# Two layernorms' inverse roots in the third layer: from one GpSimd power each to twelve VectorE instructions

## The chip, the cores and the metric

The kernel runs on one core of a Trainium2 chip. The time is the device time of one execution in microseconds; several executions of a kernel give a median. The core's engines work side by side, each with an instruction stream of its own in a fixed order, and meet only through semaphores: TensorE (PE, the matmuls), VectorE (DVE), ScalarE (ACT), GpSimd (POOL) and SyncE (SP, which only issues transfers). Indirect gathers, with rows picked by a list, are issued by GpSimd.

## The reference

The program is a network of four layers on 64 graphs of 128 nodes with 128 features, and each layer has a graph part and a feed-forward part. The change lies in the graph part of the third layer. Cut to what matters, that part and what stands around it compute:

```
# second layer, feed-forward: gates come from an attention over 524288 edges
scores = layernorm(segment_sum(h[src] * alpha, dst) + b_gat).mean over heads
x = x + sum_e gate[e] * expert_e(x)
# third layer, graph part, per node
h = layer_norm(x)                    # (x - mean) * rsqrt(var + eps); "lift", twice in a row
x = layer_norm(h' + relu(adj @ h @ W_rel + h @ W_root + b))   # "settle"
# third layer, feed-forward: a shared expert, and the best 2 of 8 routed experts
x = x + shared(x) + sum over the top two of weight * expert(x)
# fourth layer: another normalization ("ease"), attention, another norm ("blend"), experts again
```

A layernorm needs the inverse root of a variance for every node. On the chip 128 nodes lie on the 128 partitions, so a tile of roots has 128 rows and one column for each graph (twice as many for `lift`, which folds two norms in a row into one pair of factors).

## The kernel before

The program has an early part (first two layers, up to about 1543 us) and `phase_c`, the rest. In phase C the 64 graphs are worked on in 8 turns of 8 graphs (`PAIR`), each turn in 2 groups of 4 graphs (`GT`), 16 groups in all. A piece of work is a task with a name and a number, and the tasks that matter here are these:

- `rows` (GpSimd: gathers of edge rows) and `edge` (VectorE, with ScalarE): the second half of the edge attention, 16 batches. The gathers for a batch wait until the batch two before it is used. `late` (VectorE: `settle_half`, L252, and `half_gates`, L2815) turns the sums into gates for the upper 32 graphs. Turns 4 to 7 can't begin before it.
- `sum` (VectorE): adds the gated experts of the second layer to a turn. `lift`, `lift_end`, `climb`, `enter_end`: the first norm of a turn. `adj`, `xt` (transposes at L429), `agg`, `conv` on TensorE; `settle` and `settle_end`: the second norm, of a group. `f2_score`, `route`, `mark`, `list`: routing.
- `pull` (GpSimd, two gathers at L2161): fetches the tokens of an expert pass. `flip` (TensorE, L2332) transposes them, `raise` is the first matmul of a pass and `lower` the second (both recorded at L2207), and `take` (VectorE, L2623) reads the result. There are two sets of banks, so `lower` number m waits for `take` number m - 2. There are 170 routed passes and 32 of the shared expert. `gather` and `gather_last` (GpSimd, L2176) fetch the results back, four gathers a task; `ease` and `blend` are the two norms of the fourth layer.

The first half of a norm is `measure` on VectorE: mean and variance by hardware statistics, then variance plus epsilon. The root was made by `invert` on GpSimd, at L2149, a power of -0.5, and VectorE waited for it in `set_factors`, where mean and root become the factors that ScalarE applies. `inverse_root` (L235) is a helper that exists already and is used in `half_gates`; every one of its instructions waits for the one before it (`link`).

The order in which each engine works through its tasks is not written by hand: `engine_orders` (L676) is a greedy planner. It takes for each task a list of engines with estimated durations (`LONG`, L1848), the tasks that it needs (`work_c`), and a worth: the length of the longest chain behind the task, plus offsets from a table (`PREFER_C`, L1864). From these it simulates the five engines and fixes one order for each. The table `LONG` thus sets the order of the whole phase.

## Time and profile before

| | us |
|---|---|
| median of 3 runs | 2917.36 |
| lowest and highest of them | 2911.76, 2921.22 |
| the profiled execution | 2921.49 |
| its span in the trace | 2919.7 |
| TensorE busy | 2277.4 (78%) |
| VectorE busy | 1896.5 (65%) |
| ScalarE busy | 1348.5 (46%) |
| GpSimd busy | 1326.9 (45%) |

The profiled execution is one more run, with the hardware profiler on; its time and its span differ by what lies before the first and after the last instruction. The granted TensorE clock was 0.881 of full speed on average. The busy shares are averages over a program whose stages have different limits, so they don't by themselves say what a change in one stage is worth.

### The profile page before, as it was taken

The numbers are of one execution on the slowest core, as the hardware profiler recorded it, in microseconds if no ns is written. First come the engines' busy times: TensorE is split into PE (matmuls) and PEld (weight loads), VectorE is DVE, ScalarE is ACT, GpSimd is POOL, SyncE is SP. The second block draws the span as 40 slices with busy tenths as digits, with TensorE's granted clock in tenths as the row PEclk, the third lists the DMA queues.
The fourth block names the chain that finished last, engine by engine and source line by source line (L and its number), as shares of the span: only waits on it lengthen the run. The fifth ranks groups of instructions, "written<-read, shape, count | busy, mean of one in ns | idle before, by whom it ended". The sixth has DMA issues, their size and how long they took to land. (4 is left out here: it accounts for less than half of the span.)

```text
span 2919.7 us, 41767 instructions
## 1 busy us (share of the span) xinstructions
PE 2277.4 (78%) x12088; PEld 1682.4 (58%) x12088; DVE 1896.5 (65%) x4776; ACT 1348.5 (46%) x2980; POOL 1326.9 (45%) x1219
## 2 busy tenths in 40 slices
PE   4887898989888979687741617578999998999990
PEld 3443454545545445455531516568888888898980
DVE  5989988776878757555467674387465476665312
ACT  3444556554646444344421515345646544454440
POOL 1120101010101066656774667722745747767776
PEclk9988989989898979899975758689999999999995
DMA  4010101000100021422223224134635536565772
GB/s 151 1 38 0 31 1 31 4 27 1 31 5 27 18 44 29 122 78 72 73 53 114 57 65 107 38 98 115 173 92 148 163 82 183 144 152 148 180 163 75
DMA packets 282613, 228.68 MB, mean 78 GB/s; under 512 B 90042, under 2 KB 234412, under 8 KB 281468
## 3 DMA queue, kind: packets, MB, share of 16 engines
q1 hardware_dynamic: 247580, 179.75, 21.2%
q0 software_dynamic: 34784, 46.03, 8.2%
q8 instruction: 104, 1.70, 0.2%
q14 instruction: 145, 1.19, 0.1%
HBM read 163.20 MB, written 63.70 MB: 78 GB/s over the span
## 5 line engine op out<-in xcount | busy, mean ns | idle before, releaser
L983 POOL TENSOR_TENSOR a_rstd<-a_var,minus_half 128x4 f32<-128x4 f32 x64 | 120.9, 1888 | 919.0 <-DVE a_var L1529 911.7
L1627 DVE TENSOR_TENSOR room<-room 128x1024 f32<-128x1024 f32 (+1 forms) x356 | 489.8, 1391 | 24.5 <-ACT room L1373 14.6
L2161 POOL DMA_INDIRECT c_slots<-sent,c_tokens_of_slots x340 | 354.1, 1041 | 196.1 <-PE bank L2332 97.8
L2426 ACT ACTIVATE weights_f<-bank,c_expert_b 128x256 f32<-128x256 f32 x680 | 277.1, 471 | 193.5 <-PE bank L2207 192.6
L2207 PE MATMUL bank<-c_experts_w,weights_f 128*128 x2720 | 346.4, 283 | 18.9 <-ACT weights_f L2426 11.4
L2207 PEld LDWEIGHTS bank<-c_experts_w,weights_f 128*128 128x128 f32 x2720 | 337.3, 199 | 31.5 <-issue 27.5
L2207 PE MATMUL bank<-c_slots_t,c_expert_w 128*128 128x256 f32 x1360 | 340.6, 395 | 17.6 <-ACT weights_f L2426 8.3
L2207 PEld LDWEIGHTS bank<-c_slots_t,c_expert_w 128*128 128x128 f32 x1360 | 254.4, 197 | 54.2 <-issue 19.9
L1013 PE MATMUL bank<-a_h1p,weights_a 128*128 128x512 f32 x544 | 250.2, 608 | 3.0 <-ACT a_dist_exp L1350 3.0
L2623 DVE TENSOR_TENSOR c_made<-bank,c_expert_b 128x256 f32<-128x256 f32 x170 | 72.1, 424 | 258.0 <-PE bank L2207 233.9
L80 POOL DMA_INDIRECT got_room<-table_dram,own_rows x184 | 191.5, 1041 | 75.6 <-issue 75.6
L80 POOL DMA_INDIRECT room<-table_dram,own_rows x178 | 181.2, 1018 | 93.7 <-issue 93.7
L1013 PE MATMUL bank<-a_xt,weights_a 128*128 128x512 f32 (+1 forms) x352 | 203.3, 672 | 17.8 <-DVE a_conv L1570 7.0
L1013 PEld LDWEIGHTS bank<-weights_f,a_h 128*128 128x128 f32 x1024 | 129.9, 204 | 102.4 <-issue 53.6
L1013 PE MATMUL bank<-weights_f,a_h 128*128 128x128 f32 x1024 | 139.6, 293 | 56.3 <-DVE a_results L1594 42.7
L1013 PEld LDWEIGHTS bank<-a_h1p,weights_a 128*128 128x128 f32 x544 | 103.0, 195 | 121.0 <-issue 114.8
L1332 ACT ACTIVATE a_h<-bank,cols 128x512 f32<-128x512 f32 x128 | 87.0, 687 | 146.6 <-PE bank L1013 146.2
L2176 POOL DMA_INDIRECT got_room<-made,c_places x128 | 131.4, 1027 | 38.7 <-issue 37.5
L2176 POOL DMA_INDIRECT room<-made,c_places x128 | 130.6, 1020 | 39.0 <-issue 37.2
L1013 PE MATMUL bank<-spare_tiles,weights_f 128*128 128x512 f32 x256 | 130.7, 623 | 16.0 <-ACT a_h L1332 15.9
L2416 ACT ACTIVATE c_slots_t<-bank 128x256 f32<-128x256 f32 x170 | 65.7, 386 | 131.7 <-PE bank L2332 129.4
L1013 PEld LDWEIGHTS bank<-weights_a,a_h 128*128 128x128 f32 x768 | 99.1, 197 | 39.7 <-issue 17.0
(530 smaller groups left out, 4519.7 us busy)
## 6 DMA issues: line engine op xcount, KB each, us to landing
c_expert_w<-in_weights_c SPq DMA_DIRECT2D x170, 256.0 KB
made<-c_made SPq DMA_DIRECT2D x170, 128.0 KB
results_dram<-a_results SPq DMA_DIRECT2D x64, 256.0 KB
room<-results_dram SPq DMA_DIRECT2D x16, 1024.0 KB, 7.7
c_expert_b<-in_f_b SPq DMA_DIRECT2D x170, 64.0 KB
room<-in_adj SPq DMA_DIRECT2D x32, 256.0 KB, 5.3
sent<-c_rows_to_send SPq DMA_DIRECT2D x32, 256.0 KB, 3.5
c_slots<-sent,c_tokens_of_slots POOLq DMA_INDIRECT x340
```

Of the source, the lines that this page charges most:

```text
L80: pool.indirect_dma_start(out=dst, out_offset=None, in_=env.rows_dram, in_offset=bass.IndirectOffsetOnAxis(ap=index, axis=0), bounds_check ...
L983: rstd.did(g_.tensor_tensor(st.rstd[:, :], st.var[:, :], env.minus_half[:, 0:GT], ALU.pow), what, k)
L1013: return nc.tensor.matmul(out, lhsT=lhsT, rhs=rhs, start=start, stop=stop, skip_group_check=True)
L1332: sca.did(go(HV[c % 4][:, :], (U1, U2)[c % 2][:, :], ACT.Gelu, bias=env.col("f1_b1", c)), "v1", k)
L1627: v.tensor_tensor((dv[:, :, 0, :], other(dv))[j], sv[:, :, 0, :], other(sv), (ALU.min, ALU.max)[j]).then_inc(sort_step, 1)
L2161: pool.indirect_dma_start(out=XS[p.r % S_BUFS][:, j, :], out_offset=None, in_=env.sent_dram[p.q], in_offset=bass.IndirectOffsetOnAxis(ap=T ...
L2176: pool.indirect_dma_start(out=rooms[turn % 2][:, c, t, :], out_offset=None, in_=env.made_dram[q], in_offset=bass.IndirectOffsetOnAxis(ap=P ...
L2207: return nc.tensor.matmul(out, lhsT=lhsT, rhs=rhs, start=start, stop=stop, skip_group_check=True)
L2416: go(XST[p.r % 2][:, :], XB[:, 0:SLOT], ACT.Copy).then_inc(flip_copied, 1)
L2426: go(H[p.m % 2][:, c, :], U[c // 2][:, (c % 2) * SLOT:(c % 2 + 1) * SLOT], func, bias=bias).then_inc(hidden, 1)
L2623: ins = v.tensor_tensor(YB[p.r % Y_BUFS][:, :, :], y, bcast(B2[p.r % W_BUFS][:, :], [P, SLOT_TILES, D], 1), ALU.add)
```

## The change

The roots of `lift` and `settle` are made in `measure` on VectorE, by `inverse_root`: a first guess from the bits of the number (`ROOT_BITS` minus half of them), and three Newton steps (`ROOT_STEPS`). GpSimd keeps the roots of `ease` and `blend`. VectorE no longer waits in `set_factors`. The planner's table gets new durations for the two tasks, and only VectorE's queue in them.

```diff
--- before.py
+++ after.py
@@ -1847,9 +1847,9 @@
 
 LONG = {
     "rows": [(POOL, 7.5)], "edge": [(DVE, 3.9), (ACTE, 0.4), (DVE, 4.1)], "late": [(POOL, 0.3), (DVE, 19.0), (ACTE, 0.3), (DVE, 13.0)],
-    "load2": [(SP, 2.0)], "sum": [(DVE, 2.25)], "lift": [(DVE, 2.7), (POOL, 3.2)], "lift_end": [(DVE, 0.3), (ACTE, 3.9)], "climb": [(ACTE, 3.9)], "enter_end": [(DVE, 2.5)],
+    "load2": [(SP, 2.0)], "sum": [(DVE, 2.25)], "lift": [(DVE, 4.9)], "lift_end": [(DVE, 0.3), (ACTE, 3.9)], "climb": [(ACTE, 3.9)], "enter_end": [(DVE, 2.5)],
     "adj": [(PE, 0.6), (ACTE, 0.75)], "xt": [(PE, 0.6), (ACTE, 0.75)], "agg": [(PE, 1.35), (ACTE, 0.7)], "conv": [(PE, 2.2)],
-    "settle": [(DVE, 2.2), (POOL, 1.3)], "settle_end": [(DVE, 0.2), (ACTE, 1.95)], "f2_xt": [(PE, 0.6), (ACTE, 0.75)], "f2_score": [(PE, 0.9), (DVE, 0.3)],
+    "settle": [(DVE, 4.2)], "settle_end": [(DVE, 0.2), (ACTE, 1.95)], "f2_xt": [(PE, 0.6), (ACTE, 0.75)], "f2_score": [(PE, 0.9), (DVE, 0.3)],
     "route": [(DVE, 4.5), (ACTE, 0.3), (PE, 0.5), (DVE, 6.0)], "mark": [(DVE, 3.0), (PE, 0.9)], "list": [(DVE, 0.3)], "save": [(SP, 0.5)], "pull": [(POOL, 2.6)], "gather": [(POOL, 5.2)], "gather_last": [(POOL, 5.2)],
     "load3": [(SP, 2.0)], "back": [(DVE, 4.5)], "ease": [(DVE, 2.6), (POOL, 1.9)], "ease_end": [(DVE, 2.2)],
     "g3_xt": [(PE, 0.6), (ACTE, 0.75)], "project": [(PE, 1.0), (ACTE, 0.6)], "compare": [(PE, 1.1)], "mask": [(DVE, 4.6)], "soften": [(ACTE, 2.0)],
@@ -1860,6 +1860,7 @@
 LANDS = {"rows": 2.5, "load2": 6.0, "load3": 6.0, "save": 3.0, "pull": 2.5, "gather": 2.5, "gather_last": 2.5, "fetch": 5.0, "experts": 15.0, "store": 3.0}
 PIECES = 4
 NORMS = ("lift", "settle", "ease", "blend")
+POOL_ROOTS = ("ease", "blend")
 WHOLE_C = ("edge", "late", "route")
 PREFER_C = {
     "adj": (-148.0, -240.0), "agg": (215.0, 35.0), "back": (-127.0, 39.0), "blend": (31.0, 14.0), "blend_end": (-147.0, -85.0),
@@ -1979,10 +1980,10 @@
     stored_by = lambda q, k: 16 * sum(p.q <= q and p.r % Y_BUFS == k for p in routed)
     at_c = offsets(W_C)[0]
     at_col = offsets(COLS)[0]
-    measured_at = {piece: n + 1 for n, piece in enumerate(p for p in orders[DVE] if p[0] in NORMS)}
+    measured_at = {piece: n + 1 for n, piece in enumerate(p for p in orders[DVE] if p[0] in POOL_ROOTS)}
     factors_at = {piece: n + 1 for n, piece in enumerate(p for p in orders[DVE] if p[0] in ("lift_end", "settle_end"))}
     applied_at = {piece: n + 1 for n, piece in enumerate(p for p in orders[ACTE] if p[0] in ("lift_end", "climb"))}
-    inverted_at = {piece: n + 1 for n, piece in enumerate(p for p in orders[POOL] if p[0] in NORMS)}
+    inverted_at = {piece: n + 1 for n, piece in enumerate(p for p in orders[POOL] if p[0] in POOL_ROOTS)}
     marks = mark_list()
 
     with ExitStack() as ctx:
@@ -2041,6 +2042,7 @@
         RSTD = {r: sb("rstd_%s_%d" % r, [P, roots[r[0]]]) for r in norm_rooms}
         SHIFT = {r: sb("shift_%s_%d" % r, [P, roots[r[0]]]) for r in norm_rooms if r[0] in ("lift", "settle")}
         RAISE = sb("one_and_rstd", [P, PAIR])
+        ROOT = [sb(f"root_{n}", [P, 2 * PAIR]) for n in ("half", "square")]
 
         step, var_ready, rstd_ready = sem("vector_step"), sem("var_ready"), sem("rstd_ready")
         results_in, adj_in, mask_in = ([sem(f"{n}_{s}") for s in range(STREAMS)] for n in ("results_in", "adj_in", "mask_in"))
@@ -2188,7 +2190,7 @@
                     pair_rows(pool, env, R.rows[b % 2], HALF // AT_TILES + b, piece, edge_rows_in[b % 2])
                 elif what == "late":
                     further_gathers(pool, env, env.further_room, 1)
-                elif what in NORMS:
+                elif what in POOL_ROOTS:
                     invert(what, k)
                 elif what == "pull":
                     pull(routed[k])
@@ -2449,11 +2451,15 @@
                 link(ins)
                 if what == "lift":
                     v.tensor_scalar(VAR[r][:, PAIR:], MV[r][:, :, 1], 1.0 + LN_EPS, LN_EPS * LN_EPS, ALU.mult, ALU.add)
-                v.tensor_scalar(VAR[r][:, 0:tall[what]], MV[r][:, :, 1], LN_EPS, None, ALU.add).then_inc(var_ready, 1)
+                ins = v.tensor_scalar(VAR[r][:, 0:tall[what]], MV[r][:, :, 1], LN_EPS, None, ALU.add)
+                if what in POOL_ROOTS:
+                    ins.then_inc(var_ready, 1)
+                else:
+                    link(ins)
+                    link(inverse_root(nc, link, RSTD[r][:, :], VAR[r][:, :], ROOT[0][:, 0:roots[what]], ROOT[1][:, 0:roots[what]]))
 
             def set_factors(what, k):
                 r = own(what, k)
-                dve.wait_ge(rstd_ready, inverted_at[what, k])
                 if what == "lift":
                     v.tensor_scalar(RAISE[:, :], RSTD[r][:, 0:PAIR], 1.0, None, ALU.add)
                     v.scalar_tensor_tensor(SHIFT[r][:, PAIR:], MV[r][:, :, 0], -1.0, RSTD[r][:, PAIR:], ALU.mult, ALU.mult)
```

The helper, the same before and after:

```python
    link(v.tensor_scalar(bits, x.bitcast(I32), 1, None, ALU.logical_shift_right))
    link(v.tensor_scalar(out.bitcast(I32), bits, -1.0, float(ROOT_BITS), ALU.mult, ALU.add))
    link(v.tensor_scalar(half, x, -0.5, None, ALU.mult))
    for step in range(ROOT_STEPS):
        link(v.tensor_tensor(square, out, out, ALU.mult))
        link(v.tensor_tensor(square, square, half, ALU.mult))
        ins = v.scalar_tensor_tensor(out, square, 1.5, out, ALU.add, ALU.mult)
```

Since `LONG` changes, all engines get another order in phase C. Line numbers of phase C are 2 to 6 higher in the changed kernel. Three places follow; in each the rows are one instruction, or several alike, in the engine's order.

GpSimd, at the end of the gathers for edge batch 15 (the last one before `late`). Before:

```order
L98 COMPARE_AND_BRANCH
L80 DMA got_room<-table_dram,own_rows 128x24 x10
L98 UNCONDITIONAL_BRANCH
L2149 TENSOR_TENSOR c_rstd_settle<-c_var_settle,minus_half 128x4 x2
L2161 DMA c_slots<-sent,c_tokens_of_slots 128x128 x8
L288 TENSOR_LOAD tile_rounds
L288 ISA x2
L289 COMPARE_AND_BRANCH
```

In the changed kernel:

```order
L80 DMA got_room<-table_dram,own_rows 128x24 x8
L98 COMPARE_AND_BRANCH
L80 DMA got_room<-table_dram,own_rows 128x24 x10
L98 UNCONDITIONAL_BRANCH
L288 TENSOR_LOAD tile_rounds
L288 ISA x2
```

L80 are edge gathers, L2161 pulls of tokens, and L288 is the start of GpSimd's part of `late`. The pair of powers, for settles 6 and 7, is gone, and so are the eight gathers of four pulls between the batch and `late`: 16 pulls stood ahead of it, and 12 do now.

VectorE, around settle 6 and 7. Before, ahead of edge batch 15 (L138 is its first instruction):

```order
L2500 SCALAR_TENSOR_TENSOR x<-bank,x 128x512
L2445 BN_STATS ln_stats<-x 128x6 x4
L2448 BN_AGGR c_mv_settle<-ln_stats 128x2 x4
L2452 TENSOR_SCALAR c_var_settle<-c_mv_settle 128x4
L2623 TENSOR_TENSOR c_made<-bank,c_expert_b_1 128x256
L2623 TENSOR_TENSOR c_made<-bank,c_expert_b_2 128x256
L2460 SCALAR_TENSOR_TENSOR c_shift_settle<-c_mv_settle,c_rstd_settle 128x4
L138 TENSOR_SCALAR got_room<-own_rows 128x46
```

In the changed kernel settle 6 stands behind `late`, whose last instruction is the reduction into `gates`:

```order
L2850 TENSOR_REDUCE gates<-got_room 128x32
L2506 SCALAR_TENSOR_TENSOR x<-bank,x 128x512
L2447 BN_STATS ln_stats<-x 128x6 x4
L2450 BN_AGGR c_mv_settle<-ln_stats 128x2 x4
L2454 TENSOR_SCALAR c_var_settle<-c_mv_settle 128x4
L240 TENSOR_SCALAR c_root_square<-c_var_settle 128x4
L241 TENSOR_SCALAR c_rstd_settle<-c_root_square 128x4
L242 TENSOR_SCALAR c_root_half<-c_var_settle 128x4
L244 TENSOR_TENSOR c_root_square<-c_rstd_settle 128x4
L245 TENSOR_TENSOR c_root_square<-c_root_square,c_root_half 128x4
L246 SCALAR_TENSOR_TENSOR c_rstd_settle<-c_root_square,c_rstd_settle 128x4
L244 TENSOR_TENSOR c_root_square<-c_rstd_settle 128x4
L245 TENSOR_TENSOR c_root_square<-c_root_square,c_root_half 128x4
```

Settle 6 moved from ahead of edge batch 15 to behind `late`; its root follows it at once (the first seven of its instructions are shown), and the takes of expert results that stood ahead of the batch are no longer there. In the whole order 22 takes stood ahead of `late`, and 14 do now.

TensorE, at the first transposes of turn 4 (`ident,room`, x8), which need `late`. Before:

```order
L2207 MATMUL bank<-c_experts_w,weights_f 128x128 x2
L2228 TENSOR_LOAD c_pass_expert
L2228 ISA x2
L2207 MATMUL bank<-c_slots_t,c_expert_w_0 128x256 x4
L429 MATMUL bank<-ident,room 128x128 x8
L2332 MATMUL bank<-ident,c_slots 128x128 x2
L2207 ISA
```

In the changed kernel (`ident,room` stands twice, first for the adjacency of turn 4, which doesn't need `late`, then for its features):

```order
L2209 MATMUL bank<-c_experts_w,weights_f 128x128 x2
L429 MATMUL bank<-ident,room 128x128 x8
L2209 MATMUL bank<-c_xt,weights_kept 128x256 x4
L2209 MATMUL bank<-weights_kept,weights_f 128x128 x8
L2209 MATMUL bank<-bias_parts,bias_ones 128x256
L2209 MATMUL bank<-c_xt,weights_kept 128x256 x4
L429 MATMUL bank<-ident,room 128x128 x8
L2209 MATMUL bank<-weights_kept,weights_f 128x128 x8
L2209 MATMUL bank<-bias_parts,bias_ones 128x256
L2209 MATMUL bank<-room 128x128 x8
```

Ahead of those transposes stand now 13 first and 13 second matmuls of routed passes where there were 16 and 15, of the shared expert 15 and 13 where there were 16 and 16, and 15 transposed token tiles where there were 16.

## Rows read from the trace of the kernel before

**Rows 1.** the page: its first line
```profile
span 2919.7 us, 41767 instructions
```

**Rows 2.** busy time by stretches: us, busy and instructions of each engine, PEclk, DMA
```profile
1543.00:1925.00 382.00, 174.43 (x1034) 153.25 (x1034) 236.64 (x708) 132.12 (x285) 253.79 (x236) 0.70 0.28 75
1925.00:1953.00 28.00, 27.30 (x171) 25.14 (x172) 21.47 (x80) 15.73 (x41) 5.18 (x3) 0.90 0.50 149
1953.00:2609.00 656.00, 610.22 (x4199) 558.29 (x4199) 405.55 (x1305) 349.54 (x875) 388.34 (x363) 0.96 0.53 138
2609.00:2845.00 236.00, 224.02 (x1540) 206.16 (x1538) 85.24 (x264) 113.06 (x288) 182.56 (x179) 0.99 0.67 164
```

**Rows 3.** TensorE's waits, 1543 to 1925: us in total, times, longest us
```profile
PE bank L429 <- ACT c_rows_to_send L2386: 44.3, 6, 19.7
```

**Rows 4.** timeline of TensorE: start us, us, instruction [idle before, releaser]
```profile
1885.35 1.12 PE L429 MATMUL bank<-ident,c_rows_to_send 128*128 128x128 f32 x4 [19.66 <-ACT c_rows_to_send L2386]
...
1952.84 1.09 PE L429 MATMUL bank<-ident,room 128*128 128x128 f32 x8
```

**Rows 5.** the line of GpSimd's powers: duration ns min/median/max, first and last start
```profile
L2149 POOL TENSOR_TENSOR c_rstd_settle<-c_var_settle,minus_half x16: 997/1046/1085, 1602.2 to 2142.5; 128x4 f32<-128x4 f32 x16
...
L2149 POOL TENSOR_TENSOR c_rstd_lift<-c_var_lift,minus_half x8: 2930/2942/3020, 1572.3 to 2081.6; 128x16 f32<-128x16 f32 x8
```

**Rows 6.** timeline of VectorE, 1852 to 1930
```profile
1853.73 0.69 DVE L2500 SCALAR_TENSOR_TENSOR x<-bank,x 128x512 f32<-128x512 f32 x1
...
1855.78 0.17 DVE L2452 TENSOR_SCALAR c_var_settle<-c_mv_settle 128x4 f32<-128x4 f32 x1
...
1883.45 0.16 DVE L2460 SCALAR_TENSOR_TENSOR c_shift_settle<-c_mv_settle,c_rstd_settle 128x4 f32<-128x4 f32 x1 [22.92 <-POOL c_rstd_settle L2149]
...
1891.52 0.88 DVE L2623 TENSOR_TENSOR c_made<-bank,c_expert_b 128x256 f32<-128x256 f32 x2
...
1894.90 0.45 DVE L258 TENSOR_SCALAR att_den<-att_den 128x128 f32<-128x128 f32 x1 [2.08 <-issue]
...
1901.15 0.18 DVE L240 TENSOR_SCALAR got_room<-got_room 128x32 int32<-128x32 int32 x1
...
1903.83 0.69 DVE L2831 TENSOR_TENSOR got_room<-got_room 128x512 f32<-128x512 f32 x1
...
1923.36 1.22 DVE L2844 TENSOR_REDUCE gates<-got_room 128x32 f32<-128x1024 f32 x1
```

**Rows 7.** GpSimd, 1705 to 1883 by groups, then two pieces of its timeline
```profile
L80 POOL DMA_INDIRECT got_room<-table_dram,own_rows x102 | 106.5, 1044 | 39.7 <-issue 39.7
L2161 POOL DMA_INDIRECT c_slots<-sent,c_tokens_of_slots x24 | 25.0, 1043 | 7.1 <-issue 7.1
L2149 POOL TENSOR_TENSOR c_rstd_lift<-c_var_lift,minus_half 128x16 f32<-128x16 f32 x2 | 5.9, 2934 | 0.1
L2149 POOL TENSOR_TENSOR c_rstd_settle<-c_var_settle,minus_half 128x4 f32<-128x4 f32 x3 | 3.1, 1032 | 0.0
...
1705.07 1.13 POOL L80 DMA_INDIRECT got_room<-table_dram,own_rows  x1 [9.01 <-issue]
...
1882.30 2.03 POOL L2149 TENSOR_TENSOR c_rstd_settle<-c_var_settle,minus_half 128x4 f32<-128x4 f32 x2
```

**Rows 8.** timeline of VectorE: the first routing
```profile
1683.85 0.29 DVE L401 TENSOR_REDUCE c_top_max<-c_logits 128x16 f32<-128x128 f32 x1
...
1696.12 0.19 DVE L138 TENSOR_SCALAR got_room<-own_rows 128x46 f32<-128x46 int32 x1
```

**Rows 9.** the chain that ended last, 2297 to 2304: start us, us, what
```profile
2297.39 3.51 PE bank L2207 x24
...
2301.12 3.51 PE bank L2207 x24
```

**Rows 10.** timeline of GpSimd: its last pull and its last gather
```profile
2824.75 1.00 POOL L2161 DMA_INDIRECT c_slots<-sent,c_tokens_of_slots  x1 [0.30 <-issue]
...
2909.02 1.01 POOL L2176 DMA_INDIRECT room<-made,c_places  x1 [0.30 <-issue]
```

## The prediction

> **What bounds the kernel now.** I read the page first, to place the span [rows 1]: 2919.7 us, in an execution of 2921.49. Then the busy time by stretches, cut where the third layer's part ("phase C" in the code) starts, at 1543 us [rows 2]. In 1543 to 1925 TensorE is busy for 174.43 of 382 us; in 1925 to 1953 for 27.30 of 28; in 1953 to 2609 for 610.22 of 656; in 2609 to 2845 for 224.02 of 236. Then it is done, and GpSimd's last gathers and VectorE's last sums fill the rest. So TensorE's work is the bound from 1925 on, and whatever it has not done by then is added behind. Up to 1953 it idles for 382 - 174.43 + 28 - 27.30 = 208 us, after that for 46 + 12 us. The question of this change is thus what happens to those 208 us.
>
> The waits of TensorE there put 44.3 us on rows of the normed result, one of them 19.7 us long [rows 3]. What ends the starved stretch is `late`: the gates of the upper 32 graphs, which only exist when the sixteenth edge batch is done, and without which turn 4 of 8 can't be summed. TensorE's first transpose of turn 4 starts at 1952.84 [rows 4]. I call that moment X: before X TensorE lives on turns 0 to 3 and the expert passes they feed, behind X it never starves.
>
> **The roots themselves.** GpSimd's 16 powers of 128x4 take 1046 ns (median) and its 8 of 128x16 take 2942 ns [rows 5]: 16.7 + 23.5 = 40 us of its time are removed. VectorE gets 24 x 12 = 288 linked instructions. VectorE already runs this very chain, on 128x32: twelve instructions from 1901.15 to 1903.83 [rows 6], 2.68 us. The new tiles are 128x4 and 128x16; the smallest VectorE rows are 0.16 to 0.18 us long [rows 6], so 12 x 0.17 = 2.0 is the lower bound and 2.68 the upper one. I take 2.4 us for each, 58 us on VectorE in all (48 to 64). VectorE is busy for 405.55 of 656 us and 85.24 of 236 us in the stretches that TensorE bounds [rows 2], so there this lies beside TensorE's work, as long as no instruction that TensorE waits for stands right behind it; uncovered it would be the 58 us.
>
> The latency of one root, from variance to root, was 1.04 or 2.94 us when GpSimd was free; it is now 2.4. That is a loss of 1.4 us for a group and a gain of 0.5 for a turn, both small. What is large is GpSimd's queue. Settle 6's variance was ready at 1855.95 [rows 6], but its power stood behind the gathers of edge batch 15, and started at 1882.30 [rows 7]. VectorE stood still for 22.92 us until 1883.45 with edge batch 15 behind that wait [rows 6], and TensorE for 19.66 us until 1885.35 [rows 4]. That wait goes. What is late next is the data: batch 15's last gather ends where those powers start, at 1882.30 [rows 7], so VectorE's work on it couldn't have started much more than 1 us sooner. The 22.92 us are therefore no gain by themselves; only what GpSimd's queue gains is.
>
> The Trainium skill ("GPSIMD Engine Reference", section 4.1) puts elementwise work of two inputs on VectorE, at about twice GpSimd's speed. The trace agrees for one instruction but not for this exchange, since one power of 1046 ns is traded for twelve instructions of 2.4 us.
>
> **The start of `late`.** GpSimd runs without a gap from 1705.07 to the end of batch 15's gathers: 102 edge gathers, 24 pulls, and 9.0 us of powers [rows 7]. Ahead of it, 9.01 us were lost waiting for edge batch 8. In the new order on VectorE edge batches 8 and 9 stand ahead of the first routing, where 8 batches did before; the routing takes from 1683.85 to 1696.12, 12.3 us [rows 8]. So that wait goes, and so do the powers: 9.0 + 9.0 us, and the 2 us pair behind. I expect batch 15's gathers to end near 1862 in place of 1882.3. Then edge batch 15 (1883.6 to 1891.5, 8.0 us [rows 6]), a score, and `late` from 1894.90 to 1924.58, 29.7 us [rows 6]: it now starts near 1873 and ends near 1903, some 20 us sooner.
>
> **What stands around it.** The diff also changes the planner's prices, and with them the order of the phase on all engines. This is where I differ from the plain reading. Before, 22 expert results had been taken by VectorE ahead of `late`, and settles 6 and 7 too; now it is 14, and settle 6 comes right behind `late` (the VectorE rows in the section on the change). TensorE's seventeenth second matmul of a pass needs a bank that the fifteenth take frees, so TensorE stops there until `late` (1903), settle 6 (2.1, from 1853.73 to 1855.88 [rows 6]) with its root (2.4) and that take (0.4) are through: about 1908.5. From there to the first transpose of turn 4 the new order has ten second matmuls, ten first ones, seven token tiles to transpose and a few scores. By the period of a pass in TensorE's steady stretch, 24 instructions in 3.51 us plus a transpose of 0.22 [rows 9], ten passes are 37 us, and the sends, adjacency transposes and scores some 8 more, with 1 or 2 of waiting: X comes at 1955, 2 us later than before, although `late` was 20 us sooner.
>
> Ahead of X, TensorE has by then done less. By count of the order, before: 16 first and 15 second matmuls of routed passes, 16 and 16 of shared ones, 16 token tiles transposed. Now: 13 and 13, 15 and 13, and 15. At 0.146 us an instruction (3.51 / 24) and 8 instructions for a first matmul, 16 for a second, that is (3 + 1) x 8 + (2 + 3) x 16 = 112 instructions or 16.4 us, and 1 us for the transpose and the bias matmuls: 17.4 us of work moved behind X. So TensorE idles for 208 + 17.4 + 2 = 227 us up to X. That is **19 us more**, and from X on it is the bound as before.
>
> **After X.** The pairs of settles, 4.3 us of VectorE before, become about 9, and a lift grows by 2.4. A take that falls behind such a block is late by the difference, while TensorE has two banks, about one pass of 3.73 us, in hand [rows 9]. I price this at 2 us in the likeliest case; the bounds are 0 and 5 pairs x 4.8 + 4 lifts x 2.4 = 34 us. The tail is the same in both orders: behind the last pull at 2824.75 there are 64 gathers to 2909.02 [rows 10], all in the same order, and GpSimd has no settle or lift power there to lose. It shifts with TensorE.
>
> **Does VectorE's work slow the gathers?** In the stretch from 1705 to 1883, with VectorE's edge work beside them, 102 gathers took 1044 ns on average [rows 7], where one in the quiet tail takes 1.00 us [rows 10]: 4.5 us in all for everything VectorE did in 178 us. Ten roots ahead of `late` are 24 us of VectorE work, which in that proportion cost 0.6 us. The Trainium skill ("SBUF — State Buffer", section "SBUF: two separate sides") calls the port pair of VectorE and GpSimd an exclusive lock, held for a whole instruction, by VectorE instructions with two SBUF inputs among others. By that rule each of the nine such instructions of a root could hold back a gather by up to its 0.17 us: 10 x 9 x 0.17 = 15 us, which would take back most of what `late` gains and give about 2936 + 13 = 2949. The rows don't bear it out at that size, so I give it 0.04.
>
> **Sum.** 2921.49 + 17.4 + 2 + 2 = 2943 for the profiled execution. That one stood at the top of the three runs, 4.1 us over their median of 2917.36, so my number for the median is 2917.4 + 21 = **2938**.
>
> **The rivals, with chances.**
> - The forecast, slower by 8 to 30 us: 2925 to 2947. 0.46.
> - VectorE's longer blocks hold up the takes in the stretch that TensorE bounds. For it: 58 us more on an engine whose results TensorE waits for, linked, so nothing slips between. Against: VectorE is busy for only 62% there. It decides once a block is longer than the pass of lead, 3.73 us, at most of the 5 pairs. Price up to 34 us on top of 19: 2947 to 2972. 0.16; and the lock on the port, 0.04, about 2949.
> - Faster: the planner's new order lets turn 4 follow `late` closely. If TensorE's order costs nothing (the ten passes ahead of X run during `late`, because takes slip in earlier than I have them), X comes 20 us sooner, at 1933: 2897. With half of it, 2907. For it: one queue less between norm and transposes, and TensorE's 19.66 us wait gone. It decides if TensorE is less than 190 us idle ahead of X. 0.20.
> - No change: the 20 us of `late` and the 17.4 us behind X cancel, X coming near 1936 with less work done. 2909 to 2926. 0.14.
>
> **How the numbers follow.** A measurement of this kernel tells 0.3%, 9 us, from no change. Slower by more: 0.46 + 0.20 = 0.66. Within: 0.14. Faster: 0.20. The range for 8 in 10 leaves out half of the faster case at the low end and the upper half of the second at the high end: 2903 to 2962. The likeliest case's own range is 2925 to 2947.
>
> **What would show it.** In the profile after: GpSimd has no power of 128x4 or 128x16 of lift and settle, and each root is twelve instructions on VectorE in 2.0 to 2.7 us. Batch 15's last gather is issued near 1862; `late` starts near 1873 and ends near 1903; TensorE is idle through most of `late` and starts again near 1908. X is at 1955 and TensorE's idle time up to it is 227 us; behind X its idle time stays near 58 us. GpSimd's last pull is near 2845. I am wrong if X comes before 1945 (the faster case), if TensorE is idle for over 75 us between X and its end (the second), or if the gathers' mean length rises above 1.1 us (the lock).

## The result: 40 us slower

The changed kernel takes 2957.03 us (median of 5 runs, 2954.83 to 2974.34) where the kernel before takes 2916.82 (5 runs beside it, 2911.76 to 2921.22). The ratio is 1.0142, with a 95% interval of 1.0122 to 1.0163. The direction is right, and the time lies in the range for 8 in 10 (2903 to 2962). But it lies outside the likeliest case's own range (2925 to 2947), in that of the second rival (2947 to 2972, chance 0.16), and the change is about twice the 21 us that were forecast. The profiled execution is the 2974.34 us one, so 17 us of what its trace shows more is its own.

Below, M is the start of VectorE's root in the first half's gates, the last fixed point ahead of phase C: 1513.5 us in the trace of before, 1515.5 in that of after. Times "after M" can be compared between executions. X is, as in the prediction, TensorE's first transpose of turn 4 that needs `late`.

The page's first line and the busy time by stretches, in the changed kernel (up to X, two stretches of 150 us, the rest of TensorE's work; columns as in [rows 2]):

```profile
span 2972.3 us, 42029 instructions
...
1545.00:1965.80 420.80, 183.90 (x1087) 164.03 (x1088) 280.09 (x923) 135.25 (x304) 231.16 (x224) 0.68 0.26 72
1965.80:2115.80 150.00, 131.48 (x934) 119.62 (x933) 110.07 (x415) 80.50 (x199) 49.36 (x49) 0.97 0.47 130
2115.80:2265.80 150.00, 137.13 (x950) 126.46 (x948) 83.57 (x272) 80.36 (x195) 69.20 (x65) 0.94 0.45 116
2265.80:2897.00 631.20, 593.23 (x3956) 540.78 (x3957) 327.14 (x1033) 311.55 (x789) 437.64 (x420) 0.95 0.58 150
```

TensorE is busy for 183.90 us up to X, in 1087 recorded instructions; before it was 201.7 us in 1205 [rows 2]. That is the work that the new order puts behind X, and TensorE is idle for 420.8 - 183.9 = 237 us there, where it was 208. X itself comes at 1965.82, 450.3 us after M; before, at 1952.84, it was 439.3. TensorE in the timeline (start, length, instruction, idle time before and what ended it):

```profile
1875.26 3.47 PE L2209 MATMUL bank<-c_xt,weights_kept 128*128 128x256 f32 x8 [26.24 <-ACT c_xt L2347]
...
1900.39 3.75 PE L2209 MATMUL bank<-c_xt,weights_kept 128*128 128x256 f32 x8 [15.42 <-ACT weights_f L2428]
...
1917.10 3.75 PE L2209 MATMUL bank<-weights_kept,weights_f 128*128 128x128 f32 x16 [5.24 <-DVE x L2625]
...
1965.82 1.04 PE L429 MATMUL bank<-ident,room 128*128 128x128 f32 x8
```

It stands still for 26.24 us ahead of 1875.26, while VectorE waits for batch 15's rows: that is what has become of the wait of 19.66 us of [rows 4]. Then it stands still for 15.42 us during `late` and for 5.24 us behind it. After the last of these, sixteen matmuls of 128x128 take 3.75 us, where they take 1.95 at full clock (shown below). VectorE at the same place:

```profile
1871.71 0.35 DVE L141 TENSOR_TENSOR got_room<-got_room,own_rows 128x184 f32<-128x184 f32 x1 [22.66 <-DMA got_room<-table_dram,own_rows]
...
1881.84 0.23 DVE L258 TENSOR_SCALAR att_den<-att_den 128x128 f32<-128x128 f32 x1 [2.02 <-issue]
...
1910.09 1.22 DVE L2850 TENSOR_REDUCE gates<-got_room 128x32 f32<-128x1024 f32 x1
...
1914.15 0.17 DVE L240 TENSOR_SCALAR c_root_square<-c_var_settle 128x4 int32<-128x4 int32 x1
...
1916.54 0.88 DVE L2625 TENSOR_TENSOR x<-x,bank 128x256 f32<-128x256 f32 x2
```

It waits for batch 15's gathered rows for 22.66 us, where it had waited 22.92 us for the power [rows 6]. The wait changed its name, and the data is what is late next, as the prediction said. `late` runs from 1881.84 to 1911.31, which is 395.8 us after M and 15 us sooner than before. The root of settle 6 takes from 1914.15 to 1916.54, 2.39 us. GpSimd, by groups from 1705 to 1873, then the wait for edge batch 8:

```profile
L80 POOL DMA_INDIRECT got_room<-table_dram,own_rows x98 | 102.6, 1047 | 31.5 <-issue 31.5
L2163 POOL DMA_INDIRECT c_slots<-sent,c_tokens_of_slots x24 | 24.2, 1007 | 7.3 <-issue 6.7 <-PE bank L2334 0.6
...
1699.99 0.99 POOL L80 DMA_INDIRECT got_room<-table_dram,own_rows  x1 [6.48 <-issue]
```

The powers of [rows 7] are gone from the list, but a wait of 6.48 us for VectorE is left of the 9.01, and the gathers end at 1870.6, which is 355.1 us after M and 13.7 us sooner than before; 348.5 after M (1862) was forecast. Their mean length is 1047 ns, as before.

### The profile page after: what moved, and what is told of

Same layout as the page of the kernel before. It is cut to its first block and busy times, and to the rows that moved or that the text cites. A ratio compares the mean times of both kernels' runs of the same rounds, so it can differ in the third digit from the quotient of the medians.

```text
span 2972.3 us, 42029 instructions
## 1 busy us (share of the span) xinstructions
PE 2291.7 (77%) x12088; PEld 1694.3 (57%) x12088; DVE 1949.4 (66%) x5064; ACT 1346.1 (45%) x2978; POOL 1284.6 (43%) x1195
## 5 line engine op out<-in xcount | busy, mean ns | idle before, releaser
L2209 PE MATMUL bank<-c_slots_t,c_expert_w 128*128 128x256 f32 x1360 | 348.2, 402 | 8.3 <-ACT weights_f L2428 2.9
L80 POOL DMA_INDIRECT got_room<-table_dram,own_rows x184 | 190.9, 1037 | 100.5 <-issue 100.5
L80 POOL DMA_INDIRECT room<-table_dram,own_rows x178 | 180.4, 1014 | 95.7 <-issue 95.7
```

Of the source, the lines that this page charges most:

```text
L80: pool.indirect_dma_start(out=dst, out_offset=None, in_=env.rows_dram, in_offset=bass.IndirectOffsetOnAxis(ap=index, axis=0), bounds_check ...
L2209: return nc.tensor.matmul(out, lhsT=lhsT, rhs=rhs, start=start, stop=stop, skip_group_check=True)
```

## The experiments

Each was timed in five rounds beside the kernel before. The edits are shown cut to the pieces that matter. All times and ratios in one table; "late", X and the last column are from each kernel's own profiled execution, one for each kernel, so small differences in them can't be read: behind X, e6_early_half, e7_two_roots and e12_six_roots have the instructions of the kernel before, and yet 969.2 to 971.3 us for its 966.9.

| kernel | median us | ratio, 95% interval | late ends after M | X after M | X to end |
|---|---|---|---|---|---|
| before | 2916.8 | | 411.1 | 439.3 | 966.9 |
| changed | 2957.0 | 1.0142, 1.0122 to 1.0163 | 395.8 | 450.3 | 1006.5 |
| e1_old_order | 2947.7 | 1.0111, 1.0093 to 1.0130 | 422.5 | 451.1 | 991.8 |
| e2_new_order_pool | 2952.0 | 1.0125, 1.0107 to 1.0142 | 401.4 | 452.4 | 990.8 |
| e3_short_roots | 2939.7 | 1.0081, 1.0067 to 1.0095 | 386.1 | 436.8 | 996.8 |
| e4_early_power | 2956.8 | 1.0141, 1.0120 to 1.0163 | 399.2 | 454.1 | 993.9 |
| e5_late_half | 2942.1 | 1.0085, 1.0072 to 1.0098 | 410.8 | 439.3 | 993.4 |
| e6_early_half | 2927.3 | 1.0039, 1.0022 to 1.0056 | 424.2 | 452.7 | 969.6 |
| e9_load_only | 2956.1 | 1.0128, 1.0114 to 1.0143 | 428.4 | 457.0 | 992.7 |
| e10_free_roots | 2916.9 | 1.0000, 0.9990 to 1.0010 | 410.2 | 438.2 | 974.1 |
| e11_root_at_factors | 2947.8 | 1.0117, 1.0097 to 1.0137 | 423.8 | 453.0 | 989.5 |
| e12_six_roots | 2913.4 | 0.9993, 0.9983 to 1.0003 | 407.0 | 435.8 | 969.2 |
| e7_two_roots | 2917.7 | 1.0011, 1.0001 to 1.0020 | 412.1 | 440.9 | 971.3 |
| e13_new_order_free | 2938.4 | 1.0066, 1.0046 to 1.0087 | 383.7 | 434.3 | 992.4 |

### Order and load apart

**The order theory** came out of the prediction: the loss is the new order. Its rival, **the load theory**, says that it is the 58 us more on VectorE. The first experiment keeps the roots on VectorE and gives the planner its old prices:

```diff
-    "lift": [(DVE, 4.9)]
+    "lift": [(DVE, 2.7), (POOL, 3.2)]
-    "settle": [(DVE, 4.2)]
+    "settle": [(DVE, 2.2), (POOL, 1.3)]
```

> Roots of lift and settle on VectorE as in the changed kernel, but the planner keeps the old prices, so every engine keeps the order of the kernel before (GpSimd's order only loses the 24 powers). Order theory (the loss comes from the new order, which puts less of TensorE's work ahead of turn 4): late ends 10 to 20 us sooner than before with all 15 and 16 second matmuls still ahead of turn 4, so TensorE's idle time up to turn 4 falls to about 190 to 200 us and the time is 2895 to 2910 us. Load theory (the loss comes from 58 us more linked work on VectorE, which delays what TensorE waits for): slower than before also in the old order, 2930 to 2960 us.

2947.7 us, 32 over the kernel before in its rounds (2915.9): the order theory fails as the only cause, and the load costs 32 us in an order that is not changed. The second does the reverse, on the kernel before, with the new prices and the powers put back into GpSimd's order:

```diff
+    orders, done = engine_orders(work_c(), WHOLE_C, PREFER_C)
+    ends = lambda piece: done[piece] - LANDS.get(piece[0], 0.0)
+    for piece in sorted((p for p in orders[DVE] if p[0] in ("lift", "settle")), key=ends):
+        at = next((n for n, p in enumerate(orders[POOL]) if ends(p) > ends(piece) + HOP and p[0] != "late"), len(orders[POOL]))
+        orders[POOL].insert(at, piece)
```

> The new order on all engines, but the roots stay powers on GpSimd, each put into GpSimd's order where the planner had the variance ready. Order theory: as slow as the changed kernel or slower, 2950 to 2985 us, since the powers also stand among the edge gathers again. Load theory: back near the kernel before, 2915 to 2930 us.

2952.0 us: the order costs 36 us without any load. `late` ends 10 us sooner than before and X comes 13 us later. The powers stand here where the rule above puts them and not where a planner would, so this is the price of the new order with powers at these places. So there are two causes, and together they cost 40 us, not 68. The load was then taken from the new order in two steps. One Newton step in place of three:

```diff
-                    link(inverse_root(nc, link, RSTD[r][:, :], VAR[r][:, :], ROOT[0][:, 0:roots[what]], ROOT[1][:, 0:roots[what]]))
+                    link(inverse_root(nc, link, RSTD[r][:, :], VAR[r][:, :], ROOT[0][:, 0:roots[what]], ROOT[1][:, 0:roots[what]], 1))
```

> The changed kernel with one Newton step in place of three for lift and settle: 6 linked instructions a root less, 24 x 1.2 = 29 us of VectorE work less in all; the roots are coarser by that. Order theory: at most 1 or 2 roots between late and turn 4 count, so 2950 to 2957 us. Load theory: half of the loss goes, about 2937 us.

2939.7 us, 17 us less for some 29 us less of VectorE work. And a single reciprocal for a root:

```diff
-                    link(inverse_root(nc, link, RSTD[r][:, :], VAR[r][:, :], ROOT[0][:, 0:roots[what]], ROOT[1][:, 0:roots[what]]))
+                    link(v.reciprocal(RSTD[r][:, :], VAR[r][:, :]))
```

> The changed kernel's order, with one VectorE instruction (a reciprocal, so the values are not the reference's) in place of the twelve of a root. It prices the new order without its load. Twelve instructions gave 2957 us, six 2940: if that goes on in a line, two of them give about 2928 us, still 10 us over the kernel before, which would be the order's own price (17.4 us of TensorE's work behind turn 4's first transpose, less what late gains). If the order alone costs what it cost with the powers on GpSimd (36 us): 2945 us or more. If the order costs nothing: 2910 to 2918 us.

2938.4 us. The line from twelve to six instructions doesn't go on to one: against the kernel before in each one's own rounds 2 us more are gained, and the intervals overlap. What is left, 22 us, is the price of the order alone, with no root to speak of on either engine. (The reciprocal is not the root, so the values are wrong and tokens may go to other experts; the trace has the 12088 instructions on TensorE of the kernel before, and e10_free_roots below, with the same wrong values, takes the time of the kernel before.) Its stretches, up to X and behind it:

```profile
1542.00:1946.80 404.80, 180.64 (x1087) 161.42 (x1088) 255.89 (x780) 135.20 (x304) 232.96 (x224) 0.69 0.28 75
1946.80:2096.80 150.00, 143.14 (x1055) 133.55 (x1054) 103.80 (x356) 94.08 (x232) 57.92 (x57) 0.99 0.51 144
2096.80:2246.80 150.00, 133.12 (x893) 121.70 (x892) 76.75 (x241) 72.69 (x175) 64.68 (x60) 0.93 0.45 113
2246.80:2863.00 616.20, 580.73 (x3917) 529.89 (x3916) 319.36 (x1002) 307.95 (x778) 435.24 (x417) 0.96 0.59 151
```

Up to X TensorE has the 1087 records of the changed kernel. X comes 5 us sooner than before, but 992.4 us remain behind it in place of 966.9: the 17.4 us of moved work and 8 more (4 to 6 more by the rows of e6_early_half, e7_two_roots and e12_six_roots). `late` ended 27 us sooner than before, and TensorE's order could use 5 of them.

So in the new order the steps are these: 36 us with powers on GpSimd, 22 with no roots, 40 with VectorE's. Taking the powers out of the edge gathers is worth 14 us here (`late` ends at 383.7 after M in place of 401.4), and VectorE's roots cost 19.

Where do they cost them? The execution of the changed kernel that the profiler took is 17 us over the median, so e4_early_power (below), which differs by a single small power and took 2956.1 us in its profiled execution, is the better witness. Up to X, and behind it:

```profile
1535.40:1960.00 424.60, 181.51 (x1088) 162.21 (x1089) 280.21 (x923) 135.17 (x304) 230.11 (x225) 0.69 0.27 71
1960.00:2110.00 150.00, 132.01 (x932) 120.42 (x931) 109.53 (x412) 79.95 (x198) 48.27 (x49) 0.95 0.46 129
2110.00:2260.00 150.00, 141.29 (x998) 131.00 (x996) 88.21 (x294) 85.20 (x207) 71.97 (x67) 0.97 0.49 124
2260.00:2882.00 622.00, 588.85 (x3944) 538.38 (x3943) 324.16 (x1015) 308.47 (x780) 435.78 (x420) 0.95 0.59 151
```

From e13_new_order_free to this kernel `late` moves by 15.5 us (383.7 to 399.2 after M) and X by 19.8, but the rest behind X only from 992.4 to 993.9; TensorE's idle time behind X is 922 - 862.1 = 60 us, as in the kernel before (58). In the new order the load is thus mostly paid ahead of X, as far as one execution of each can tell. The profiled execution of the changed kernel itself has 1006.5 us and 69 us of idle time there, so how much it can cost behind X varies from one execution to the next; the medians of the two kernels are equal.

### The load alone, and the relief alone

The kernel before, with twelve instructions on a scratch tile more for each root that GpSimd still makes:

```diff
+                if what in ("lift", "settle"):
+                    link(inverse_root(nc, link, ROOT[2][:, 0:roots[what]], ROOT[3][:, 0:roots[what]], ROOT[0][:, 0:roots[what]], ROOT[1][:, 0:roots[what]]))
```

> The kernel before with its powers on GpSimd and its order, and twelve linked VectorE instructions of a root on a scratch tile more behind each variance, whose result nobody reads. It is the load alone. If VectorE's load is what costs: as slow as the old order with VectorE's roots or slower, since GpSimd is not relieved, 2947 to 2965 us. If the relief of GpSimd or the loss of the early power setting plays the part: below 2935 us.

2956.1 us, 38 us over the kernel before (2917.9 in its rounds): the load alone. That is 6 us more than the 32 with GpSimd relieved (e1_old_order), by ratios whose intervals overlap. The other side, the old order with the reciprocal of e13_new_order_free (the diff of e1_old_order and that one together):

> Order of the kernel before, and one VectorE instruction (a reciprocal, so the values are not the reference's) in place of the twelve of a root, none on GpSimd. It is GpSimd's relief with next to no load. Place theory: edge batches follow one another without delay and 9 us of powers leave the gathers ahead of late; late ends some 10 us sooner, 2900 to 2912 us, the most that moving the roots could bring in this order. If GpSimd's relief is worth nothing: 2915 to 2920 us.

2916.9 us, a ratio of 1.0000. With next to no load, freeing GpSimd from all 24 powers, 40 us of its time, brings nothing in this order; I had expected 2900 to 2912 us. Its trace shows two small effects that cancel. From the end of the 9 us wait for edge batch 8 to the last gather of batch 15 GpSimd needs 171.1 us in place of 177.2, with its powers gone. But that wait ends 3.6 us later after M, with one linked instruction for each root more in VectorE's queue ahead of it. `late` ends 1 us sooner.

### Where the load costs

The old order, on the kernel before, with the predicate `on_pool` deciding for each root where it is made (the line for the turns 0 to 3; the places that ask it are left out):

```diff
+def on_pool(what, k):
+    return what in NORMS and k < {"lift": 4, "settle": 8}.get(what, 99)
```

> Order of the kernel before; roots on VectorE only for turns 4 to 7 (lift 4 to 7, settle 8 to 15), GpSimd's powers for turns 0 to 3. Place theory (VectorE is gapless from 1562 to 1723 us, so each of the first turns' roots delays edge batches and late, and behind turn 4 the longer VectorE blocks delay what TensorE waits for): late and the first transpose of turn 4 as in the kernel before, only the part behind grows, by 10 to 20 us: 2926 to 2937 us. Uniform theory (each root costs the same wherever it stands, 31.7 us / 24 = 1.3 us): 12 roots, 2932 us, but with late later too.

And its mirror image:

```diff
+    return what in NORMS and (what in ("ease", "blend") or k >= {"lift": 4, "settle": 8}[what])
```

> The mirror image: order of the kernel before, roots on VectorE only for turns 0 to 3 (lift 0 to 3, settle 0 to 7). Place theory: late ends 8 to 12 us later against the end of the first part, the stretch behind turn 4's first transpose stays at some 967 us: 2925 to 2930 us, and with the late half it adds up to the 31.7 us of both. If GpSimd's freed queue were the path to late, late would be sooner and the time 2905 to 2915 us.

2942.1 and 2927.3 us: 24 and 9 us over the kernel before beside them. The sum, 33.5, is what all roots cost in this order (31.7), so the halves add up. The uniform theory falls, since 12 roots cost 24 us in one half and 9 in the other, and the table's columns say where: the early half moves X by 13 us and leaves the rest (969.6), the late half leaves X at 439.3 and adds 26.5 us behind it.

**Ahead of X.** The first stretch of phase C up to the moment when VectorE first waits for gathered rows, in the old order with VectorE's roots (busy times by engine, then GpSimd's waits, from a view that begins 15 us earlier: total, times, longest):

```profile
1548.50:1727.00 178.50, 70.04 (x408) 61.36 (x408) 135.71 (x449) 54.58 (x115) 87.23 (x85) 0.66 0.19 50
...
POOL got_room L80 <- issue: 96.0, 97, 13.5
```

The same in the kernel before, with its stretches behind X for what follows:

```profile
1560.00:1723.00 163.00, 66.95 (x408) 58.17 (x408) 122.91 (x378) 54.64 (x115) 99.33 (x91) 0.69 0.21 55
...
POOL got_room L80 <- issue: 49.2, 97, 9.0
POOL c_rstd_lift L2149 <- DVE c_var_lift L2452: 12.3, 1, 12.3
POOL c_rstd_settle L2149 <- DVE c_var_settle L2452: 6.9, 3, 5.5
...
1952.80:2102.80 150.00, 138.19 (x1007) 127.67 (x1006) 97.66 (x348) 88.34 (x217) 79.03 (x71) 0.99 0.50 132
2102.80:2252.80 150.00, 140.60 (x979) 127.95 (x980) 79.87 (x232) 83.02 (x200) 72.32 (x67) 0.98 0.49 125
2252.80:2845.00 592.20, 555.65 (x3754) 508.99 (x3752) 313.44 (x990) 291.44 (x748) 419.55 (x405) 0.96 0.60 153
```

163 us have become 178.5. VectorE does 71 instructions more, six roots, at 2.4 us each some 14.4 us; GpSimd is busy for 12 us less and idle for 178.5 - 87.2 = 91 us in place of 163 - 99.3 = 64. (Its waits are 96.0 us in place of 68.4: 49.2 ahead of gathers and 19.2 ahead of powers.) VectorE is busy for 122.91 of the 163 us, its linked instructions leave short pauses between them, and the edge batches stand in its queue. So here GpSimd waits for VectorE and a root on VectorE is on the path to `late`. A power of GpSimd is on it only behind 1705 us, where the gathers follow one another without a gap [rows 7].

**Behind X**, in e5_late_half:

```profile
1531.00:1940.80 409.80, 202.64 (x1204) 179.14 (x1204) 259.67 (x798) 147.59 (x326) 255.92 (x238) 0.71 0.29 80
1940.80:2090.80 150.00, 128.34 (x900) 118.42 (x901) 104.89 (x396) 77.14 (x187) 55.47 (x54) 0.94 0.44 122
2090.80:2240.80 150.00, 136.43 (x939) 123.45 (x938) 89.94 (x304) 82.76 (x203) 65.12 (x60) 0.96 0.47 118
2240.80:2859.00 618.20, 584.00 (x3904) 535.19 (x3904) 320.97 (x1002) 302.80 (x774) 433.98 (x417) 0.94 0.59 151
```

In the 300 us behind X TensorE does 900 + 939 records where the kernel before does 1007 + 979, and then both keep their pace. The totals behind X are 5743 and 5740 records, in 848.8 and 834.4 us of busy time and 69.4 and 57.8 us of idle time. The 26 us are thus 12 us of waiting and 14 us of the same matmuls taking longer, at a granted clock of 0.94 and 0.96 in the two stretches of 150 us, and 0.94 after them, for 0.99, 0.98 and 0.96. A part of the 14 is the one execution of the kernel before: TensorE's stretch behind X in e6_early_half, e7_two_roots and e12_six_roots, where nothing has changed, is

```profile
1959.90:2855.20 895.30, 839.93 (x5753) 769.82 (x5752) 492.20 (x1568) 463.19 (x1163) 572.44 (x542) 0.96 0.56 144
...
1945.00:2844.20 899.20, 842.71 (x5752) 773.41 (x5752) 491.88 (x1568) 461.83 (x1160) 575.04 (x544) 0.95 0.56 144
...
1939.40:2836.80 897.40, 841.54 (x5753) 770.87 (x5752) 490.71 (x1568) 463.35 (x1163) 573.16 (x544) 0.96 0.56 144
```

and to the same last instruction e5_late_half has

```profile
1940.80:2860.60 919.80, 850.37 (x5752) 778.53 (x5752) 515.80 (x1700) 462.69 (x1163) 555.87 (x532) 0.94 0.55 140
```

Against these three it has 13 to 14 us more of idle time and 8 to 10 us more of busy time, together the 24 us of the medians or a little less. The largest wait is at the first norms of turn 4. VectorE there (the root of lift 5 starts at 1949.26, of settle 8 at 1954.02, of settle 9 at 1958.75; the last row is settle 8's factors):

```profile
1949.06 0.16 DVE L2455 TENSOR_SCALAR c_var_lift<-c_mv_lift 128x8 f32<-128x8 f32 x1
1949.26 0.17 DVE L240 TENSOR_SCALAR c_root_square<-c_var_lift 128x16 int32<-128x16 int32 x1
...
1954.02 0.17 DVE L240 TENSOR_SCALAR c_root_square<-c_var_settle 128x4 int32<-128x4 int32 x1
...
1958.75 0.17 DVE L240 TENSOR_SCALAR c_root_square<-c_var_settle 128x4 int32<-128x4 int32 x1
...
1961.13 0.16 DVE L2469 SCALAR_TENSOR_TENSOR c_shift_settle<-c_mv_settle,c_rstd_settle 128x4 f32<-128x4 f32 x1
```

And the same place before, from the last variance of the lift to settle 8's factors:

```profile
1961.08 0.16 DVE L2452 TENSOR_SCALAR c_var_lift<-c_mv_lift 128x8 f32<-128x8 f32 x1
...
1965.77 0.15 DVE L2460 SCALAR_TENSOR_TENSOR c_shift_settle<-c_mv_settle,c_rstd_settle 128x4 f32<-128x4 f32 x1
```

4.7 us have become 12: three roots in a row stand ahead of the factors of settle 8. What TensorE makes of it, in its timeline and then in busy times with the granted clock (the column behind GpSimd's):

```profile
1963.03 1.12 PE L429 MATMUL bank<-ident,c_rows_to_send 128*128 128x128 f32 x4 [7.62 <-ACT c_rows_to_send L2389]
1964.56 3.02 PE L2210 MATMUL bank<-c_experts_w,weights_f 128*128 x16 [0.41 <-ACT weights_f L2429]
...
1973.87 1.95 PE L2210 MATMUL bank<-c_experts_w,weights_f 128*128 x16
...
1963.00:1965.00 2.00, 1.56 (x6) 1.17 (x7) 0.00 (x0) 2.00 (x6) 0.00 (x0) 0.50 0.54 134
1965.00:1967.00 2.00, 2.00 (x13) 2.00 (x13) 0.00 (x0) 2.00 (x7) 0.00 (x0) 0.59 0.65 187
1967.00:1969.00 2.00, 2.00 (x14) 1.82 (x13) 0.42 (x1) 2.00 (x7) 0.00 (x0) 1.00 0.14 41
```

It waits for 7.62 us, and then the granted clock is 0.50 of full speed, the lower of two levels (1.2 GHz), for some 3.5 us, and 1.00 (2.4 GHz) from 1967 on. Sixteen instructions take 3.02 us behind the wait and 1.95 further on. So this wait cost its own length and, as an estimate from these rows, one or two us more behind it.

That block was taken apart by making each root where its factors are made, in the old order:

```diff
             def set_factors(what, k):
                 r = own(what, k)
+                link(inverse_root(nc, link, RSTD[r][:, :], VAR[r][:, :], ROOT[0][:, 0:roots[what]], ROOT[1][:, 0:roots[what]]))
```

> Order of the kernel before, all roots on VectorE, but each root is made where its factors are made (set_factors) and no longer behind its variance. Block theory (behind turn 4's first transpose VectorE makes the roots of lift 5, settle 8 and settle 9 in a row, 7 us, ahead of settle 8's factors, and TensorE waits 7.6 us for the normed rows and then runs at the lower clock for some us): 2 of the 3 roots leave that place, TensorE's wait there falls to 2 or 3 us, and the time from 2948 to 2935 or 2943 us. If the mere number of instructions counts: no change, 2945 to 2950 us.

2947.8 us, no change. The wait did fall. TensorE's waits for the normed rows are (total, times, longest), from 1950 to 2130 us here, then in the same stretch of e1_old_order:

```profile
PE bank L429 <- ACT c_rows_to_send L2388: 7.1, 3, 3.0
...
PE bank L429 <- ACT c_rows_to_send L2388: 9.7, 2, 7.6
```

The longest is 3.0 us in place of 7.6. All of TensorE's waits behind X fell too, from 70 us to 62. The time didn't follow: TensorE was busy for 4 us longer with the same work (854 for 850), X came 2 us later (453.0 after M for 451.1), and the tail behind TensorE's last instruction took 1 us more. The block theory is right on the place of that one wait and wrong on what it is worth. Why the other parts grew isn't shown, and differences of this size also stand between two executions of one kernel.

### Smaller suspects, and a version to keep

In the changed kernel GpSimd's first power in this phase comes at 2154.00 us, after 7.51 us idle. In the kernel before the first power, at 1572.28 us, comes after 12.33 us of waiting for its variance, under which such a time would not show. One power was put ahead of its work:

```diff
+            nc.gpsimd.tensor_tensor(FIRST[:, :], env.ones_nt[:, 0:1], env.minus_half[:, 0:1], ALU.pow)
```

> The changed kernel with one 128x1 power more, ahead of GpSimd's work in this phase. In the changed kernel GpSimd loads the setting for its powers only at the first ease, where it idles 7.5 us with pulls queued behind; in the kernel before that lay at 1560 us under a wait. If that costs, the time falls by up to 7 us to about 2950; if TensorE's queue of pulled tokens covers it, no change: 2955 to 2959 us.

2956.8 us: the wait costs nothing. In this trace the power of the first ease follows the pulls without idle time (2141.23), so the 7.51 us did go. The wait of 22.92 us alone, settles 6 and 7 on VectorE:

```diff
+    return what in NORMS and (what, k) not in (("settle", 6), ("settle", 7))
```

> Order of the kernel before; only the roots of settles 6 and 7 go to VectorE, the pair on which VectorE stood still for 22.9 us and TensorE for 19.7. Data theory: the batch's gathers end when they ended, so late moves by 1 or 2 us at most, TensorE's wait only moves to the next thing that needs late's takes: 2914 to 2918 us. If those waits were a cost of their own: 2900 us.

2917.7 us: nothing is gained, so the wait for the power was not a cost of its own. VectorE stands still at the same place for 18.92 us, now for the gathered rows, and TensorE for 19.63. And the six roots whose powers lay inside GpSimd's gapless gathers, made at the factors:

```diff
+    return what in NORMS and (what, k) not in (("lift", 2), ("lift", 3), ("settle", 4), ("settle", 5), ("settle", 6), ("settle", 7))
```

> Order of the kernel before; only the six roots that GpSimd made between its gapless edge gathers (lifts 2 and 3, settles 4 to 7) go to VectorE, made at the factors, where VectorE waits for gathered rows anyway; the other 18 stay powers. Place theory: 8 us of powers leave the gathers, late ends 5 to 9 us sooner, nothing changes behind: 2907 to 2914 us, faster than both kernels. If GpSimd's relief is worth nothing there either, as when all roots were nearly free: 2915 to 2920 us.

2913.4 us in 12 runs, 2.1 less than the kernel before in 23, with an interval of 0.9983 to 1.0003. GpSimd's stretch up to batch 15's last gather is 6 us shorter, as in e10_free_roots, and here its start is only 0.5 us later: `late` ends 4 us sooner and X comes 3.5 us sooner, in line with the theory's sign and a little below its size. It is the fastest of all, but it is not clear of no change.

## Why the prediction was right, and where it was off

- **The price of a root** was right: in the trace of after 2.34 to 2.65 us for settle and 2.48 to 2.73 for lift, for the 2.4 taken, 60 us in all for the 58.
- **The wait of 22.92 us is no gain by itself**: right. The data came at nearly the same moment, and e7_two_roots shows that taking the power out of it brings nothing.
- **`late` 20 us sooner**: 15 were measured (12 in e4_early_power). The step that failed is that VectorE's roots were priced at nothing ahead of `late`. The prediction counted GpSimd's queue only. But up to the wait for edge batch 8 VectorE's queue is the path. Of that wait 6.48 us were left, and with the same order and one instruction for a root `late` ends 15.5 us sooner than in e4_early_power (383.7 for 399.2 after M) and X comes 19.8 us sooner. In the old order, e6_early_half puts the early roots at 9 us (13 in the trace).
- **Batch 15's gathers near 1862**: a slip in the sum besides. The 9.0 us of powers in [rows 7] hold the first of the pair at 1882.30, and both of that pair stand behind the last gather, so they can't bring it forward: 1882.3 - 9.0 - 8.0 = 1865.3, 3 us later than the forecast had it.
- **112 instructions, and with the transposes and bias matmuls 117, move behind X**: right. The trace counts 118 fewer records. Their price of 17.4 us is that part of TensorE's busy time, 201.7 less 183.9 = 17.8.
- **X 2 us later, TensorE starting near 1908**: in e4_early_power the term that missed most. X came 11 us later after M, and 15 us later there. TensorE started behind `late` at 1917.1; 6 us of it are `late` (395.8 after M for the 389.5 reckoned), and the stretch from TensorE's start to X took 48.7 us for the 46.5 reckoned.
- **Behind X, 17.4 us of moved work and 2 us for longer blocks**: 27.0 us in e4_early_power and 39.6 in the slower trace of after. The blocks aren't what is missing in the first of these: e13_new_order_free has 25.5 us without the roots, so the moved work was priced 8 us too low, or 4 to 6 by the rows of the unchanged kernels. There was a rival for the blocks, with up to 34 us. In the old order it holds: 12 late roots cost 24 us in e5_late_half. For the changed kernel it isn't shown: the number lies in its range, but the mark set for it, over 75 us of idle time behind X, was not reached (69, and 60 in e4_early_power), and the load was mostly paid ahead of X. The mark would also have missed the half of the cost that shows as busy time in e5_late_half, since I had left out that the clock falls behind a wait.
- **The order alone**: 21 us were forecast, and 21.7 are measured with no root to speak of (e13_new_order_free). That is luck in part, since two errors cancel: X came 5 us sooner and not 2 later, and 25 us came behind it and not 19.
- **The rivals.** Faster: no experiment but e12_six_roots came below the kernel before, and that one not clearly. The lock on the port between VectorE and GpSimd, which the Trainium skill states ("SBUF — State Buffer", section "SBUF: two separate sides"), has no part that can be seen: with the roots beside them the gathers take 1047 ns on average, for 1044 before [rows 7]. The page holds it, for VectorE instructions with two SBUF inputs, only against a GpSimd operation that reads SBUF, a condition that the prediction left out.
- **VectorE as the place for elementwise work** ("GPSIMD Engine Reference" of the Trainium skill, section 4.1): not for this trade. One power of 1.05 us in GpSimd's queue became 2.4 us in the queue that more engines wait for. In the old order the load costs 38 us (e9_load_only) and the relief brings none by itself; in the new one the load costs 19 and the relief brings 14.

So the sum was half the measured change since the forecast named one cause, the order, and it was one of two. The two don't simply add (32 and 22 would be 54), and the table shows where they don't. In the old order the load costs 12 us up to X and some 21 to 25 behind it; in the new one 20 up to X and, in the execution near the median, 1 or 2 behind. What stays open is why the roots behind X cost so little in the new order. It is made for the longer tasks, which fits, but no run isolates it; nor does one say which waits of the moved order make the microseconds beyond the moved work.

## What to carry to other kernels

Before work is moved from an idle-looking engine to another, look stretch by stretch at who waits for whom: here GpSimd was busy 45% and VectorE 65% on average, but in the first 180 us of the phase GpSimd waited for VectorE. Test relief and load apart, with work that nobody reads and with work left out, and do it in each order that is compared: here the relief was worth 0 us in one and 14 in the other. And a table of durations that feeds a planner is a change of its own: it should be timed alone (here 36 us with the powers kept, 22 with no root left), and its offsets tuned again, before the edit that it describes is judged.

## What the hardware showed that was not expected

- A wait of TensorE of 5.24, 7.62 or 15.42 us was followed by matmuls at half speed for some 4 us (3.75 and 3.02 us for sixteen instructions in place of 1.95, and 3.75 for eight of 128x256 in place of 1.89), so that a part of the loss behind X stands in the column of busy time. In the trace of after the granted clock is 0.50 from 1900.4 to 1904.4 us, behind the longest of them, and 1.00 from 1907 to 1911. That all of the longer busy time in e5_late_half is the clock isn't shown.
- Leaving out half of each root's twelve instructions gained 17 us, and leaving out nearly all of the rest 2 us more at most.
